# Fewer PSUM slots per tile in a neighbour-max kernel: three shared slots a tile, fifteen members, and a path for rows that meet in one

## The reference, cut to what matters

```python
scores = jnp.where(mask, -arange(N), -inf)      # top_k: the first S=25 neighbours
vals, idx = jax.lax.top_k(scores, S)
agg = where(valid, X[idx], -inf).max(axis=2)
agg = where(degree <= S, maximum(agg, 0.0), agg)
out = relu(concatenate([X, agg], -1) @ W + b)
x = layernorm(x + out)
```

## Time and profile before

| | |
|---|---|
| median of 3 runs | 624.4 us (624.03 to 627.11) |
| the profiled execution, its own time | 624.25 us |
| its span, first to last instruction | 622.4 us |
| TensorE busy, matmul | 501.3 us, 81% |
| VectorE busy | 534.3 us, 86% |
| ScalarE / GpSimd busy | 394.6 us / 290.4 us |
| mean granted TensorE clock | 0.956 of 2.4 GHz |

### The profile page before, as it was taken

One profiled execution on the slowest core, in us unless ns is written; L12 is line 12 of the kernel. 1 busy time (PEld: TensorE's weight loads), 2 busy tenths in 40 slices (PEclk: granted clock), 3 DMA queues, 4 the chain that ended last, 5 costly groups with the idle time before them and its releaser, 6 DMA issues.

```text
span 622.4 us, 14481 instructions
## 1 busy us (share of the span) xinstructions
PE 501.3 (81%) x4480; PEld 341.9 (55%) x4544; DVE 534.3 (86%) x973; ACT 394.6 (63%) x751; POOL 290.4 (47%) x462
## 2 busy tenths in 40 slices
PE   1366997889968996889974999679987999779982
PEld 0124675566654675456752666555764567555762
DVE  4656999899898998899995998998898999998884
ACT  3361577448965688557864588665886478545744
POOL 2643365246633655146733356335552467336610
PEclk9997999899998999799997999998999999899996
DMA  8982336353434647345534445355544463021102
GB/s 244 224 221 72 102 98 129 98 153 96 134 95 137 151 115 125 106 130 143 132 97 112 133 107 137 86 141 137 135 124 120 116 141 59 18 57 36 46 10 70
DMA packets 91815, 71.38 MB, mean 115 GB/s; under 512 B 63651, under 2 KB 80294, under 8 KB 91686
## 3 DMA queue, kind: packets, MB, share of 16 engines
q1 hardware_dynamic: 85286, 56.77, 35.6%
q0 software_dynamic: 6400, 13.12, 8.4%
HBM read 50.99 MB, written 4.19 MB: 89 GB/s over the span
## 4 chain that ended last, share of the span: by engine, by line
PE 30%; DVE 22%; issue 14%; ACT 12%; DVEq 8%; DMA 7%; another core or an unknown queue 3%; POOL 1%; SPq 1%; POOLq 1%; ACTq 0%
PE pair L1037 25%; DVE part L776 11%; DMA adj_sb<-in_adj 3%; ACT row_work L712 3%; DMA g_feat<-in_x,g_idx 3%; DVE hot L771 3%; ACT mask L586 3%; DVEq L846 3%; DVEq L915 2%; ACT distance L629 2%; ACT hot L636 2%; DVE g_feat L849 2%; PE misc L1082 1%; DVE g_val L817 1%
## 5 line engine op out<-in xcount | busy, mean ns | idle before, releaser
L1037 PE MATMUL pair<-hot,x_part 128*128 128x128 bf16 (+3 forms) x3120 | 416.6, 281 | 66.0 <-DVE part L776 33.8
L1037 PEld LDWEIGHTS pair<-hot,x_part 128*128 128x128 bf16 x3120 | 239.0, 99 | 176.1 <-issue 64.0
L776 DVE TENSOR_REDUCE part<-pair 128x128 f32<-128x1024 f32 (+1 forms) x256 | 279.8, 1099 | 47.2 <-PE pair L1037 45.9
L484 POOL DMA_INDIRECT g_feat<-in_x,g_idx x200 | 192.8, 964 | 112.5 <-issue 96.0
L521 POOL TENSOR_TENSOR y_sb<-relu_sb,x_sb 128x128 f32<-128x128 f32 x64 | 32.8, 512 | 194.1 <-ACT relu_sb L647 193.8
L593 ACT ACTIVATE V<-p_V 128x512 bf16<-128x512 f32 x98 | 58.0, 592 | 93.4 <-remote 71.7
L621 ACT ACTIVATE hot<-V,first_bias 128x1024 bf16<-128x1024 bf16 x56 | 64.1, 1145 | 52.8 <-PE pair L1037 52.8
L771 DVE TENSOR_SCALAR hot<-V 128x1024 bf16<-128x1024 bf16 x224 | 84.3, 397 | 0.0
L586 ACT ACTIVATE mask<-adj_sb 128x1024 bf16<-128x1024 uint32 x56 | 58.8, 1050 | 20.5 <-DMA adj_sb<-in_adj 20.5
L636 ACT ACTIVATE hot<-distance,one 128x1024 bf16<-128x1024 bf16 x56 | 64.0, 1143 | 0.2
L629 ACT ACTIVATE distance<-V,second_bias 128x1024 bf16<-128x1024 bf16 x56 | 63.7, 1137 | 0.0
(11 more groups left out here) (88 smaller groups left out, 396.6 us busy)
## 6 DMA issues: line engine op xcount, KB each, us to landing
adj_sb<-in_adj SPq DMA_DIRECT2D x56, 512.0 KB
g_adj<-in_adj SPq DMA_DIRECT2D x8, 512.0 KB, 4.4
x_sb<-in_x SPq DMA_DIRECT2D x8, 512.0 KB, 3.9
out<-y_sb SPq DMA_DIRECT2D x7, 512.0 KB, 5.1
g_feat<-in_x,g_idx POOLq DMA_INDIRECT x200
maskT<-mask SPq DMA_TRANSPOSE x56
out<-y_sb SPq DMA_DIRECT2D x1, 448.0 KB, 3.0
w_sb<-in_W SPq DMA_DIRECT2D x1, 128.0 KB, 6.3
```

The lines of the kernel that those rows point to most:

```text
L484: pool.indirect_dma_start(out=g_feat[w][:, k, :], out_offset=None, in_=x_rows, in_offset=bass.IndirectOffsetOnAxis(ap=g_idx[w][:, k:k + 1] ...
L776: dve.tensor_reduce(part[:, par(q, s), :, p], slots_of(q, s, p).rearrange("f k i -> f i k"), AX.X, ALU.max).then_inc(s_used, 1)
L1037: last = pe.matmul(dst, x_part[:, q, part_no, kb], one_hot, start=(first and part_no == 0), stop=(final and part_no == PARTS - 1))
```

## The change

Every tile has three shared slots with fifteen members in all (before: two slots with ten members in tiles 1 to 3, three with eleven in tiles 4 to 7). That makes 200 slots a batch where there were 228, and 25 groups, all of 8 slots, where there were 32 (7 of them with 4 slots): tile 1 has five groups instead of six, tiles 2 and 3 four instead of five, tiles 4 to 7 three instead of four. The last group holds the three shared slots in its last three places. The 284 picked ranks stay, but in 186 pieces instead of 143. More rows now reach two members of one slot. For such a tile there is a level 2, `APART`: TensorE picks the fifteen members once more, each into a slot of its own in two further groups (`apart_level`: 8 and 7 slots, 45 matmuls), VectorE reduces the last group again over its first five slots only and then the two further groups (`apart_reduce`). Level 3 is both this and the two ranks more; level 4 is the redo. `EXTRACT` is moved to the new group numbers.

```diff
-SHARED = {1: (((0, 11), (3, 5), (4, 6), (5, 5), (7, 5)), ((0, 12), (1, 7), (3, 6), (4, 5), (6, 5))),
...
+SHARED = {1: (((0, 12), (2, 6), (3, 5), (4, 6), (7, 4)), ((0, 10), (1, 6), (5, 5), (6, 5), (7, 5)),
+              ((0, 11), (1, 7), (3, 6), (4, 5), (6, 4))),
...
+OWN_LAST = BANKS * BANK - SHARES
...
-    VIOLS = NT + 1 + SHARES
+    FLAGS = LEVELS + 1
+    APART, REDO = 2, 4
+    VIOLS = NT + 1
...
+            def apart_reduce(i, q, s):
+
+                dve.wait_ge(s_used, pair_no(i, q, s, COUNT[s]))
+                dve.tensor_reduce(part[:, par(q, s), :, COUNT[s] - 1], buffer_of(q, s, COUNT[s] - 1)[:, 0:OWN_LAST]
+                                  .rearrange("f k i -> f i k"), AX.X, ALU.max)
+                for p in range(EXTRA):
+                    dve.wait_ge(s_xpair, 2 * EXTRA * pos(i, q, s) + p + 1)
+                    dve.tensor_reduce(more[:, :, p], apart_slots(q, s, p).rearrange("f k i -> f i k"),
+                                      AX.X, ALU.max).then_inc(s_xused, 1)
+                dve.drain()
+                maxima = part[:, par(q, s), :, 0:EXTRA]
+                dve.tensor_tensor(maxima, maxima, more[:, :, :], ALU.max).then_inc(s_xdone, 1)
...
-                dve.scalar_tensor_tensor(out=level[:, q], in0=vsum[:, 1], scalar=float(LEVELS), in1=vsum[:, 0],
+                dve.scalar_tensor_tensor(out=unlike[:, :], in0=vsum[:, LEVELS], scalar=float(APART), in1=vsum[:, 0],
+                                         op0=ALU.mult, op1=ALU.add)
+                dve.drain()
+                dve.scalar_tensor_tensor(out=level[:, q], in0=vsum[:, 1], scalar=float(REDO), in1=unlike[:, :],
                                          op0=ALU.mult, op1=ALU.max).then_inc(s_level, 1)
...
-            EXTRACT = {1: {4: 0}, 2: {1: 1, 4: 2}, 3: {3: 3}, 4: {3: 4}, 5: {1: 5, 3: 6}, 6: {}, 7: {1: 7, 3: 8}}
+            EXTRACT = {1: {4: 0}, 2: {1: 1, 3: 2}, 3: {3: 3}, 4: {2: 4}, 5: {0: 5, 2: 6}, 6: {}, 7: {1: 7, 2: 8}}
...
                     with dve.If(lv > 0):
-                        with dve.If(lv < LEVELS):
-                            extra_hots(q, s)
-                            extra_reduce(i, q, s)
+                        with dve.If(lv < REDO):
+                            with dve.If(lv > 1):
+                                apart_reduce(i, q, s)
...
+            def apart_level(i, q, s):
+                u = par(q, s)
+                for p in range(EXTRA):
+                    pe.wait_ge(s_used, pair_no(i, q, s, COUNT[s]))
+                    members = MEMBERS[s][2 * BANK * p:2 * BANK * (p + 1)]
+                    for k, (kb, r) in enumerate(members):
+                        one_hot = hot[:, u, r - 1, kb] if r <= LOW else hot_high[:, u, r - 1 - LOW, kb]
+                        pick(apart_slots(q, s, p)[:, k], q, kb, one_hot, s_xpair if k == len(members) - 1 else None)
...
                     with pe.If(lv > 0):
-                        with pe.If(lv < LEVELS):
-                            extra_level(i, q, s)
-                            pe.wait_ge(s_xused, EXTRA * (m + 1))
+                        with pe.If(lv < REDO):
+                            with pe.If(lv > 1):
+                                apart_level(i, q, s)
+                            with pe.Else():
+                                pe.sem_inc(s_xpair, EXTRA)
+                            pe.wait_ge(s_xused, 2 * EXTRA * m + EXTRA)
```

More of the change, by code:

```diff
@@ L88, in groups @@
     filled = banks(depths, shared)
-    filled.sort(key=lambda bank: max(r + n for kb, r, n, place in bank))
-    count = -(-len(filled) // BANKS)
-    first = [len(filled) * g // count for g in range(count + 1)]
-    return [[(kb, r, n, BANK * h + place) for h, bank in enumerate(filled[first[g]:first[g + 1]])
-             for kb, r, n, place in bank] for g in range(count)]
+    filled = sorted(filled[1:], key=lambda bank: max(r + n for kb, r, n, place in bank)) + filled[:1]
+    return [[(kb, r, n, BANK * h + place) for h, bank in enumerate(filled[g:g + BANKS])
+             for kb, r, n, place in bank] for g in range(0, len(filled), BANKS)]
 def build(nc, x, adj, W, b, out):
@@ L111, in build @@
     assert FRONT == MT
+    MEMBERS = {s: [member for slot in SHARED[s] for member in slot] for s in SHARED}
+    assert all(len(MEMBERS[s]) <= EXTRA * 2 * BANK and len(SHARED[s]) == SHARES for s in SHARED)
     SLOTS = {s: [max(n + place for kb, r, n, place in group) for group in GROUPS[s]] for s in GROUPS}
@@ L115, in build @@
     assert all(sum(piece[2] for group in GROUPS[s] for piece in group) == sum(DEPTHS[s]) for s in GROUPS)
+    assert all(SLOTS[s][-1] == OWN_LAST + SHARES for s in GROUPS)
     assert all(d[HIGH_BLOCKS] <= LOW and list(d) == sorted(d, reverse=True) for d in DEPTHS.values())
```

101 lines of the change are left out of this document (63 added, 38 removed), and 4 rows, old and new, of the table SHARED.

## The result

The changed kernel takes 642.09 us (median of 4 runs, 638.81 to 647.37), the kernel before 624.95 (624.03 to 627.11): 1.028 times as long, interval 1.020 to 1.035. I had forecast 629, within 613 to 638: the direction was right, the size was missed by 13 us, and the result lies 4 us outside the range. The profiled execution took 647.37 us, with a span of 645.5; it is the longest of the four, 5 us above the median.

What follows compares the result with a forecast made beforehand. No engine alone bounds it: each batch runs through TensorE, then a gather chain to tile 6, then VectorE. 624.25 - 16.5 (shorter batches) + 21.4 (picking rows apart, with half clock) = 629.15, forecast 629 us, range 613 to 638.

Steps and rivals of the forecast that it cites:

- events: Picking apart five rows that meet in a slot, in four tiles: 17.2 us, plus 4.2 for half clock, +21.4 together.
- the ring: A batch as three stretches (TensorE, gather chain, VectorE): seven times 2.35 us saved less 0.15, -15.4 of -16.5 us.
- level to gate: From `set_levels` ahead of tile 2 to VectorE's gathered rows in tile 6: +0.15 us a batch for split picks.
- the price of the last event: Picking apart in batch 7 tile 6: 4.6 us, and 1.7 for the clock, 6.3 us.
- Reductions between gate and level: VectorE from tile 6's gathered rows to the next `set_levels`: fewer reduced slots and smaller merges, -2.35 us a batch.
- That `linear_main` now follows the last group costs nothing: TensorE's multiplication with W behind the last group: 0 us, since the ReLU waits for the copy behind it anyhow.
- Picks, 2 ns a split: TensorE's 143 pieces a batch become 186: 2 ns per split, weight loads hidden, +0.15 us a batch from tile 2 to 4.
- Rival 1: VectorE's whole saving reaches the end, as tile 6's gathered rows come earlier: 611 or 621.8 us; chance 0.28.
- Rival 2: Gains and the cost of picking apart cancel, for instance 2.7 us a batch against 5 us each: 624 us; chance 0.15.
- Rival 3: Picking apart costs 34 us in all, or VectorE is late behind the 20-rank group: 641 us; chance 0.11.
- Rival 4: TensorE's longer jump at tile ends leaves the fetched window, 0.3 us for each of 52: 645 us; chance 0.04.
- Rival 5: The count of meeting rows is wrong and picking apart doesn't run: 608 us; chance 0.02.

Runs made afterwards that it cites:

- tables by tile: Changed kernel with a shared-slot table for each tile, so no rows meet, 173 pieces a batch: 615.00 us, 0.982; on a slower chip 695.94 us, 1.026.
- the spread cuts: Kernel before with picks cut into 186 pieces a batch, cuts in the first groups of a tile: 629.72 us, 1.007.
- the change without its events: Changed kernel with shared-slot flags weighted 0, so no tile is picked apart and five rows are wrong: 718.77, 704.26, 715.99, 702.50 us on slower chips, 1.038 to 1.047.
- the repeat: Changed kernel, unedited, run again beside the kernel before at 624.67 us: 640.65 us, 1.024.
- the early release: Changed kernel in which TensorE no longer waits for VectorE's second count in tiles whose rows meet: 641.06 us, 1.026.
- the split kernel: Kernel before with picks cut into 186 pieces a batch, from the last group on: 693.15 us, 1.024, and 703.33 us, 1.019, on two slower chips.

## Why the prediction was right in its direction and wrong in its size

Chip A is the one to hold it against. The kernel with tables by tile, which has no event for rows that meet, is at 615.00 there, against 624.67, so -9.7; 13 pieces a batch more would be 1.3 us by the spread cuts. By this estimate (the change without its events didn't run on chip A) it would stand near 616, -8.4, where I had -16.5, and its events cost 24.4, where I had 21.4. Eight of the missing 13 us lie in the ring and three in the events; about one and a half is that the median of the result is above that of the later group. The direction came out because the events did outweigh the rings; both terms were off, and both to the slower side.

Two steps of the prediction failed: level to gate, put at +0.15 us a batch, and the price of the last event, put at 6.3 us with the clock.

- *Reductions between gate and level, -2.35 us a batch:* right. Six batches without the jump back give -3.5, -2.4, -2.6, -1.2, -2.0 and -2.2, mean -2.3 (tables by tile: -2.0).
- *"That `linear_main` now follows the last group costs nothing", and "from level to the end of tile 4 it stays":* this is the first step that failed. `linear_main` was harmless in tiles 4 to 7, but I had priced neither that it comes 12 matmuls later in every tile nor `rank_product`, which changed places with the last group in tiles 2 and 3. Both make GpSimd's residual of tile 2 late. I had seen that GpSimd waits 2.13 us for the ReLU of tile 3 and read it as proof that TensorE sets the gate. It was also all the slack that GpSimd had. Batches 2 to 6, which have no event, lose 7.6 us between level and gate in the result's trace and 7.8 in the repeat. With as many half-clock stretches as before (tables by tile) they lose 3.3, so less than half of the loss is shown to come from the order of work.
- *The clock in tile 2:* show 0.54 there, in one batch. In the changed kernel the next `linear_main` behind the level comes 8.3 us after it in batches 2 and 3 and 6.2 to 6.8 in batches 1, 4, 5 and 6; the kernel before has 5.4 to 6.1, and 7.5 in batch 5. The late ones are those with a granted clock of 0.56 to 0.70 behind the level. Such batches number two in the result's trace, three in the repeat, none with the early release, one with tables by tile and one before; what brings them is not shown. I had priced the half clock behind events only. There it wasn't the same each time either: behind the events of batches 0 and 1 the granted clock is 0.72 and 0.69 in the result's trace and 1.00 in the repeat. Part of what the profiled execution has above the median lies in this.
- *The rest of the ring.* In the traces the kernel with tables by tile is only 6.5 us shorter than the one before, where I had 16.5. From gate to level it gives 13.0 instead of 16.4 in seven batches, since the stretch with the jump back gives 0.9; the end of the last batch gives 0.3 instead of 1.4; level to gate costs 4.9 in all eight batches instead of 1; and the first level comes 1.9 us later instead of 0.3, a place that ranges from 49.9 to 52.0 us in the five traces of the table above.
- *The jump back:* batch 3 has +1.7 where -2.35 was due. TensorE waits 2.82 and 1.20 us for reductions in tile 7, does the 20-rank group at half clock and then has the jump, 7.05 us against 6.72:

```profile
335.59 3.95 PE L1085 MATMUL pair<-hot,x_part 128*128 128x128 bf16 x42
...
349.99 2.74 PE L1085 MATMUL pair<-hot,x_part 128*128 128x512 bf16 x6 [7.05 <-issue]
```

  In the later run on chip A that stretch is 32.9 us, so this part isn't the same each time either.
- *The events:* their number and places were right, and their sum nearly (24.4 by the estimate above and 23.0 on chip B1, against 21.4), but it hides two errors. Against the kernel with tables by tile the stretch with both events of batch 0 is 6.7 us longer in the result's trace and 6.3 in the repeat, where I had 8.4 with the clock; that of batch 1 is 8.4 and 6.5 longer, where I had 6.7; that of batch 7 is 10.5 longer in both, where I had 6.3. This is the second step that failed. From TensorE's last matmul ahead of the event to the next tile's pick it is 5.8 us in batch 0 tile 4, 6.5 in batch 1 tile 3 and 10.4 in batch 7 tile 6. Behind the gate VectorE is the engine that is late, and an event throws away TensorE's lead: it waits 3.75 us where I had 1.2, and the picks of the event and of the next tile meet the half clock. I had put this event below that of tile 3.
- *Picks, 2 ns a split:* 4.2 us in place of 2.1 on chip A, within its error; 17.5 us on chip B1. The duration of a matmul in a dense row of the trace was no bound from above for a chip that I hadn't seen.
- *Rival 1, the gate gives way:* it fell; the wait at the gate grew, from 6.7 to 12.9 us. *Rival 2* fell with the events, which cost three times what the rings gave. *Rival 3, 641 us by dearer events or a late VectorE:* nearest in time, but by chance: it had 34 us of events and full gains of the rings, and there were 24 and half the gains. Only the last event is as dear as it said. Its other half, VectorE late behind the 20-rank group, isn't what the trace shows: outside of events TensorE waits for reductions in tiles 2 to 5 for 0.6 to 0.8 us at a time, in all for less than before (29.4 us against 33.8), and VectorE waits 77.1 us for TensorE. *Rival 4, the jump:* fell by the gap of 0.43 us and the sum of 21.4. *Rival 5:* fell, since all four ran.

What stays open: what brings the half-clock stretches behind the level, what the moved `rank_product` costs by itself, why the change without events has more of the unexplained gaps than the split kernel on chip B1, and why chips B are slower at all.

## What to carry to other kernels

Where a group goes away, list every operation whose place was written relative to the group numbers, on the engine whose order is by hand, and follow each to the queue behind the next engine; the one that matters need not be the one named in the change. An engine that waits 2 us at a chain's start has 2 us of slack and no more. Before a loss in one trace is put down to an order of work, hold several executions of it against each other, with the granted clock beside each stretch; and a wait that a profile names is tested by taking it away. A rare slow path is priced by the lead that it throws away, not only by its own instructions; where a table of constants sets how often it runs, look for a better table before making the path faster: here that turned 1.024 into 0.982.

## What the hardware showed beside that

The same program takes 625 us on one chip and 675 to 688 on three others, and its verdict can turn over: tables by tile give 0.982 on the first and 1.026 (1.019 to 1.033) on one of the others. On these TensorE starts single 128-column matmuls 0.71 us apart in some dense rows and 56 ns apart in others of the same trace. Many small matmuls are thus a risk that one chip's trace doesn't show.
